# Delta rule's inversion: products, copies and masked writes over 32 of 64 columns per chunk

## The reference, cut to what matters

```
decay = jnp.tril(jnp.exp(jnp.tril(g[..., :, None] - g[..., None, :])))
tri = jnp.tril(jnp.einsum('bhnck,bhndk->bhncd', k_beta, k) * decay, -1)
eye = jnp.eye(chunk, dtype=jnp.float32)
Tm = jsl.solve_triangular(eye + tri, jnp.broadcast_to(eye, tri.shape), lower=True)
v_new = Tm @ v_beta
k_cum = Tm @ (k_beta * jnp.exp(g)[..., None])
```

## Time and profile before

| | |
|---|---|
| time, median of 3 runs | 3494.46 us (3492.59 to 3495.26) |
| profiled execution: its time, its span | 3488.75 us, 3487.0 us |
| busy: PE, PEld, DVE, ACT, POOL | 3025.8, 2083.1, 2289.0, 1233.2, 1019.2 us |
| mean granted TensorE clock | 0.944 of full speed |

### The profile page before, as it was taken

The page is one execution under the profiler, slowest core; times in us unless marked ns, Lnnn a source line. Parts: engine busy times, 40 slices in busy tenths (PEclk is TensorE's granted clock), DMA queues, the critical chain, the costliest instruction groups (busy, mean ns, idle before and its releaser), DMA issues. The chain is left out here.

```text
span 3487.0 us, 82116 instructions
## 1 busy us (share of the span) xinstructions
PE 3025.8 (87%) x33083; PEld 2083.1 (60%) x33083; DVE 2289.0 (66%) x5113; ACT 1233.2 (35%) x2979; POOL 1019.2 (29%) x1495
## 2 busy tenths in 40 slices
PE   6999998299966899889889889989989988988597
PEld 3444443166654677667667667667666766766365
DVE  4666666588835675775776666676677667665476
ACT  2333434033323333343343333333334234332354
POOL 3545556057821211212221221221221222121011
PEclk8999999599968999999999999999999999999799
DMA  2111111000001000010010010000000000000000
GB/s 80 32 33 32 34 31 27 30 1 1 1 14 39 23 25 18 17 29 20 17 29 18 19 29 17 20 18 28 20 17 29 20 17 29 17 17 2 25 19 31
DMA packets 94038, 80.40 MB, mean 23 GB/s; under 512 B 54992, under 2 KB 68320, under 8 KB 93664
## 3 DMA queue, kind: packets, MB, share of 16 engines
q1 hardware_dynamic: 93664, 75.18, 7.9%
HBM read 57.70 MB, written 4.85 MB: 18 GB/s over the span
## 5 line engine op out<-in xcount | busy, mean ns | idle before, releaser
L1643 PE MATMUL gd_bk<-gd_xT,gd_wh 128*128 128x512 f32 x768 | 416.0, 653 | 17.1 <-ACT gd_xT L1358 7.8
L1368 ACT COPY gd_O<-gd_bk 64x128 f32<-64x128 f32 x448 | 110.0, 259 | 561.2 <-PE gd_bk L1770 560.8
L1413 DVE SCALAR_TENSOR_TENSOR gd_YK<-gd_bk,gd_cw,gd_YK 128x511 f32<-128x511 f32 (+2 forms) x384 | 285.5, 743 | 18.5 <-ACT gd_YK L1290 11.9
L390 DVE TENSOR_REDUCE at_nm<-at_ring 128x2 f32<-128x256 f32 (+3 forms) x256 | 199.2, 820 | 145.9 <-PE at_ring L531 145.9
L1471 DVE COPY_PREDICATED gd_U<-gd_mU,gd_bk 128x256 f32<-128x256 int32 x320 | 140.9, 440 | 201.1 <-PE gd_bk L1836 138.3
L1379 ACT COPY gd_ZS<-gd_bk 128x256 f32<-128x256 f32 x320 | 119.1, 372 | 387.3 <-PE gd_bk L1814 379.6
L1814 PE MATMUL gd_bk<-gd_L,gd_NT 64*64 64x64 f32 x5120 | 203.7, 223 | 57.8 <-DVE gd_L L1473 57.8
L1814 PEld LDWEIGHTS gd_bk<-gd_L,gd_NT 64*64 64x64 f32 x5120 | 169.2, 134 | 112.5 <-DVE gd_L L1473 75.2
L1831 PE MATMUL gd_bk<-gd_U,gd_ZS 64*64 64x64 f32 x5120 | 203.4, 221 | 0.1
L276 POOL TENSOR_TENSOR at_PT<-at_PT,at_dm 128x1024 f32<-128x1024 f32 (+3 forms) x128 | 197.3, 1541 | 10.6
L1786 PE MATMUL gd_bk<-gd_V,gd_KK 64*128 64x128 f32 x896 | 165.8, 306 | 38.6 <-DVE gd_V L1564 38.2
(11 more groups left out here) (358 smaller groups left out, 6746.4 us busy)
## 6 DMA issues: line engine op xcount, KB each, us to landing
gd_wh<-in_L_attn_W_qkvz SPq DMA_DIRECT2D x64, 512.0 KB, 3.7
gd_gb<-gates SPq DMA_DIRECT2D x128, 64.0 KB, 3.3
X<-in_L_attn_x SPq DMA_DIRECT2D x8, 512.0 KB, 8.7
at_QT<-at_QS SPq DMA_DIRECT2D x128, 32.0 KB, 1.9
at_KT<-at_KS SPq DMA_DIRECT2D x128, 32.0 KB, 1.9
at_OC<-at_Ob SPq DMA_DIRECT2D x128, 32.0 KB, 1.9
at_RC<-inverse SPq DMA_DIRECT2D x128, 32.0 KB, 1.8
out_x<-X SPq DMA_DIRECT2D x8, 512.0 KB, 2.9
```

Of the source, the lines that this page charges most:

```text
L390: nc.vector.tensor_reduce(nm[v % 2][:, k, c0:c0 + HS + 1:HS], set_of(s, 2 + p)[:, :, 0:n], AX.X, ALU.max).then_inc(max_done, 1)
L1413: nc.vector.scalar_tensor_tensor(out[:, s:W], bank_[:, 0:W - s], cw[:, j, head(f, e), CONVK - 1 - s:CONVK - s], out[:, s:W], ALU.mult, ALU ...
L1643: ins = nc.tensor.matmul(out[:, :], wh[e][:, k, col * DK:(col + 1) * DK], xT[:, k, :], start=k == 0, stop=k == DC - 1)
```

## The change

At level l, `U` changes only in those columns whose index has bit l set (side 1), and `L` only in those where it is clear (side 0): 32 of 64 per chunk. The new helper `side` picks these columns out of a chunk as blocks of 2^l columns with as many skipped between them, `side_all` and `side_mask` do so for a whole tile, and `packed` and `packed_rows` address a part of the bank in which only such columns lie, side by side: 128 instead of 256 columns for a head. All products of the inversion now move 32 columns instead of 64, with the same 64 x 64 stationary operand; the ACT copy moves 128 x 128, and writes it in the places of side 0 of `ZS`; the masked writes on DVE are 128 x 128. The number of instructions in the inversion, their order and their semaphores stay as they are. `ZS` is set to zero once by POOL, with a wait for it on ACT; the masks are stored for four chunks (128 x 256) instead of one, since `side_mask` can't be broadcast.

```diff
@@ -877,6 +877,7 @@
     H, DK, CK = 8, P, 64
     CPT = P // CK
     NCH = N // CK
+    HC = CK // 2
     CONVK = conv_w.shape[2]
     LEVELS = 6
     W = TPS * P
@@ -900,8 +901,8 @@
         maskc, identc = sb("maskc", [P, CK]), sb("identc", [P, CK])
         jj, ii, jx = sb("jj", [P, CK], I32), sb("ii", [P, CK], I32), sb("jx", [P, CK], I32)
         m1, m2 = sb("m1", [P, CK], I32), sb("m2", [P, CK], I32)
-        mU = [sb(f"mU{l}", [P, CK], I32) for l in range(LEVELS)]
-        mL = [sb(f"mL{l}", [P, CK], I32) for l in range(LEVELS - 1)]
+        mU = [sb(f"mU{l}", [P, TPS, CK], I32) for l in range(LEVELS)]
+        mL = [sb(f"mL{l}", [P, TPS, CK], I32) for l in range(LEVELS - 1)]
         xs = sb("xs", [P, TPS, D])
         xT = sb("xT", [P, DC, W])
         mhalf = sb("mhalf", [P, 2 * TPS])
@@ -992,7 +993,8 @@
                         for src, dst in ((ii, mU[l]), (jj, mL[l] if l < LEVELS - 1 else None)):
                             if dst is not None:
                                 mask(nc.vector.tensor_scalar(m2[:, :], src[:, :], l, 1, ALU.logical_shift_right, ALU.bitwise_and))
-                                mask(nc.vector.tensor_tensor(dst[:, :], m1[:, :], m2[:, :], ALU.mult))
+                                mask(nc.vector.tensor_tensor(dst[:, :, :], m1[:, :].unsqueeze(1).broadcast_to([P, TPS, CK]),
+                                                             m2[:, :].unsqueeze(1).broadcast_to([P, TPS, CK]), ALU.mult))
                     dve.wait_ge(c_in, 6 * 16)
                     with dve.Fori(0, B) as b:
                         dve.wait_ge(gxt_mm, b * DC + 2)
@@ -1099,6 +1101,7 @@
             "z_mm", "zs_done", "y_mm", "u_done", "vk_mm", "kc_mm", "vnc_done", "kc_done", "oz_done")
         p1_mm, w_done, o1_done, ds_mm, s_done, oi_mm, o_done, ms_done, h_done, ht_mm, ht_out = per_head(
             "p1_mm", "w_done", "o1_done", "ds_mm", "s_done", "oi_mm", "o_done", "ms_done", "h_done", "ht_mm", "ht_out")
+        zs_zero = [sem(f"zs_zero{e}") for e in E2]
         gb_in = [[sem(f"gb_in{e}{i}") for i in range(2)] for e in E2]
         rk_step, rk_done, rq_step, rq_done, fac_step, fac_done = (
             sem(n) for n in ("rk_step", "rk_done", "rq_step", "rq_done", "fac_step", "fac_done"))
@@ -1153,6 +1156,26 @@
 
         def wide(m):
             return m[:, :].unsqueeze(1).broadcast_to([P, TPS, CK])
+        def side(ap, l, bit):
+            return ap.rearrange("p (b s n) -> p b s n", s=2, n=1 << l)[:, :, bit, :]
+        def side_all(tile, l, bit):
+            return tile[:, :, :].rearrange("p t (b s n) -> p (t b) s n", s=2, n=1 << l)[:, :, bit, :]
+        def side_mask(m, l, bit):
+            return m[:, :, :].rearrange("p t (b s n) -> p (t b) s n", s=2, n=1 << l)[:, :, bit, :]
+        def packed(b_, part, l):
+            return b_[:, part * TPS * HC:(part + 1) * TPS * HC].rearrange("p (b n) -> p b n", n=1 << l)
+        def packed_rows(b_, part, c, t, l):
+            return b_[rows(c), part * TPS * HC + t * HC:part * TPS * HC + (t + 1) * HC].rearrange("p (b n) -> p b n", n=1 << l)
 
         def ends_seq(q):
 
@@ -1266,6 +1289,8 @@
                     pool.wait_ge(eps_done, b + 1)
                     nc.gpsimd.tensor_tensor(rstd[:, :], rstd[:, :], mhalf[:, 0:TPS], ALU.pow).then_inc(rstd_done, 1)
 
+                for e in E2:
+                    nc.gpsimd.memset(ZS[e][:, :, :], 0.0).then_inc(zs_zero[e], 1)
                 exponents(0)
                 for q in range(-1, PAIRS):
                     f = q + 1
@@ -1376,7 +1401,9 @@
                         for e in E2:
                             if has(f):
                                 act.wait_ge(z_mm[e], f * (LEVELS - 1) + l)
-                                nc.scalar.copy(ZS[e][:, :, :], chunks(A_[e])).then_inc(zs_done[e], 1)
+                                if f == 0 and l == 1:
+                                    act.wait_ge(zs_zero[e], 1)
+                                nc.scalar.copy(side_all(ZS[e], l, 0), packed(A_[e], 0, l)).then_inc(zs_done[e], 1)
                         if l == 1 and has(f):
                             queries_first(f, 0)
                             if has(f + 1):
@@ -1462,15 +1489,15 @@
                 def first_level(f, e):
                     dve.wait_ge(nt_done[e], f + 1)
                     dve.wait_ge(ui_done[e], f + 1)
-                    nc.vector.copy_predicated(U[e][:, :, :], wide(mU[0]), NTm[e][:, :, :])
+                    nc.vector.copy_predicated(side_all(U[e], 0, 1), side_mask(mU[0], 0, 1), side_all(NTm[e], 0, 1))
                     dve.wait_ge(idz_mm[e], f + 1)
-                    nc.vector.copy_predicated(L[e][:, :, :], wide(mL[0]), chunks(F1[e])).then_inc(u_done[e], 1)
+                    nc.vector.copy_predicated(side_all(L[e], 0, 0), side_mask(mL[0], 0, 0), packed(F1[e], 0, 0)).then_inc(u_done[e], 1)
 
                 def level(f, e, l):
                     dve.wait_ge(y_mm[e], f * (LEVELS - 1) + l)
-                    last = nc.vector.copy_predicated(U[e][:, :, :], wide(mU[l]), chunks(A_[e], 1))
+                    last = nc.vector.copy_predicated(side_all(U[e], l, 1), side_mask(mU[l], l, 1), packed(A_[e], 2, l))
                     if l < LEVELS - 1:
-                        last = nc.vector.copy_predicated(L[e][:, :, :], wide(mL[l]), chunks(A_[e], 0))
+                        last = nc.vector.copy_predicated(side_all(L[e], l, 0), side_mask(mL[l], l, 0), packed(A_[e], 1, l))
                     last.then_inc(u_done[e], 1)
 
                 def attention_rows(f, e):
@@ -1708,7 +1735,7 @@
                     pe.wait_ge(nt_done[e], f + 1)
                     for t in range(TPS):
                         for c in range(CPT):
-                            last = nc.tensor.matmul(F1[e][rows(c), t * CK:(t + 1) * CK], NTm[e][rows(c), t, :], identc[rows(c), :],
+                            last = nc.tensor.matmul(packed_rows(F1[e], 0, c, t, 0), NTm[e][rows(c), t, :], side(identc[rows(c), :], 0, 0),
                                                     start=True, stop=True)
                     last.then_inc(idz_mm[e], 1)
 
@@ -1811,8 +1838,8 @@
                                     ge(pe, s_done[e], f * NCH)
                                 for t in range(TPS):
                                     for c in range(CPT):
-                                        last = nc.tensor.matmul(A_[e][rows(c), t * CK:(t + 1) * CK], NTm[e][rows(c), t, :], L[e][rows(c), t, :],
-                                                                start=True, stop=True)
+                                        last = nc.tensor.matmul(packed_rows(A_[e], 0, c, t, l), NTm[e][rows(c), t, :],
+                                                                side(L[e][rows(c), t, :], l, 0), start=True, stop=True)
                                 last.then_inc(z_mm[e], 1)
                         if l == 1 and has(f):
                             queries_in(f, 1)
@@ -1828,13 +1855,13 @@
                                 pe.wait_ge(zs_done[e], f * (LEVELS - 1) + l)
                                 for t in range(TPS):
                                     for c in range(CPT):
-                                        last = nc.tensor.matmul(A_[e][rows(c), (TPS + t) * CK:(TPS + t + 1) * CK], ZS[e][rows(c), t, :],
-                                                                U[e][rows(c), t, :], start=True, stop=True)
+                                        last = nc.tensor.matmul(packed_rows(A_[e], 2, c, t, l), ZS[e][rows(c), t, :],
+                                                                side(U[e][rows(c), t, :], l, 1), start=True, stop=True)
                                 if l < LEVELS - 1:
                                     for t in range(TPS):
                                         for c in range(CPT):
-                                            last = nc.tensor.matmul(A_[e][rows(c), t * CK:(t + 1) * CK], U[e][rows(c), t, :], ZS[e][rows(c), t, :],
-                                                                    start=True, stop=True)
+                                            last = nc.tensor.matmul(packed_rows(A_[e], 1, c, t, l), U[e][rows(c), t, :],
+                                                                    side(ZS[e][rows(c), t, :], l, 0), start=True, stop=True)
                                 last.then_inc(y_mm[e], 1)
                         if l == 4 and has(f):
                             values_across(f, 1)
```

## The result

The change makes the kernel slower. Its median is 3673.24 us (3669.5 to 3684.95, four runs), that of the kernel before beside it 3493.53 us (3487.43 to 3495.26, four runs): 1.0523 times the time, 95% interval 1.0495 to 1.0552, 180 us more. The forecast of 3442 and its range are both missed; what came is rival C, at over five times its price.

What follows compares the result with a forecast made beforehand. No engine bounded the whole inversion part: PE paced level 1 and from level 4's Z products on, DVE between. Steps summed to 1.67 us a pair, together 52 us, taking 3494.5 to 3442; range 3400 to 3490.

Steps and rivals of the forecast that it cites:

- rival C: Inversion part: PE streams half the columns, so its clock falls; 1.35 us a fall, two a pair give 3528 us; chance 0.09.
- The products. Here I expect almost nothing: Inversion products: the 64-column stationary operand keeps records 30 ns apart; only a group's last record ends about 0.03 us sooner.
- step 1: `queries_in` of head 0, waiting for a masked write, starts earlier, limited by head 1's transposes: gain 0.22 us a pair.
- step 2: End of level 1: head 1's writes end sooner, so level 2's taps and head 1's Z group start 0.30 us earlier.
- step 3: Level 2: both heads' shorter writes let the Z group of level 3 start another 0.54 us earlier.
- step 4: Level 3: both heads' writes stand on the path; Z of head 0 gains 0.27, head 1 another 0.20: 0.47 us.
- step 5: Level 4: PE sets the pace, so gain 0; the saved DVE time turns into DVE idle.
- step 6: Level 5: Y products follow the first ACT copy; 0.11 us from the copy and 0.03 from the drain give 0.14.
- Rival B: DVE's masked writes in short runs with gaps aren't shorter; some 0.2 us a pair remains, 3488 us; chance 0.08.
- Rival A: Inversion products get cheaper, 15 ns a record instead of 30; some 3.3 us a pair more, 3340 us; chance 0.06.
- The 0.03 that I took at each group's end: Last record of each product group, 223 ns, should shrink by about 0.03 us for 32 columns less.
- Costs taken as nothing: Mask products' 2.1 us on DVE covered by a 2.45 us wait for PE; POOL's zeroing of `ZS` hidden before pair 0's gates.

## Why the prediction was wrong

**The failed step** is "The products. Here I expect almost nothing". For the distance of the records it was right. But it took PE's price from the records alone and put the clock among the rivals at 0.09, with the reason that "weight loads, the busy share of PE and the gaps stay as they are". They did stay, and the clock fell all the same: in the 14.4 us ahead of the fall of pair 5 PE was busy for 12.51 us and loaded weights for 9.44, against 12.19 and 8.89 before; in the low stretch it was busy in 20.40 of 20.40 us, with a weight load for each record, and stayed at 0.50. What the runs put in place of that step is a fall of 20.4 us in 22 of the 32 parts and of about 10 in seven, 179 us net of the gain, that comes with the narrow products and with nothing else of the change. The row that could have told was in the prediction, 0.50 with PE busy for 31.3 of 36 us; 96 of its 142 records move 16 columns, the others 128. I read it as a clock that hadn't risen yet.

The Trainium skill, in TensorE: Matmul & The Clock Gate, Part 1, has the clock low by default and released by PE's activity. The busy share of the records can't be read as that activity here: it was 1.00 in the stretch at 0.50.

**Rival C** named the mechanism, the place and the sign. Its size was off, and the term that was off is the length of a fall. It took 1.35 us for one, from a scan part whose mean clock of 0.95 over 31.74 us comes to some 3.2 us at 0.50, and two falls a pair for 3528. What came was one of 20.4 us, which costs 8.7. For each us at the lower level that is about 0.42 us by the prediction's rows, and 0.43 and 0.42 in the falls of 20.4 and 10.2 us: the price was right, and a fall over six times as long made the loss. The prediction said "more if the clock stays down" and gave that no number.

**The steps of the sum.** For pair 14, at full clock in both kernels, I compared the starts of PE's groups counted from the start of the part. The gain had reached 0.06 us at the first `queries_in` (step 1 said 0.22); 0.16 at head 1's Z group of level 2 (step 2: another 0.30, got 0.10); 0.83 at head 1's Z group of level 3 (step 3: another 0.54, got 0.67); 1.08 at the Z groups of level 4 and 1.18 at the Y groups behind them (step 4: another 0.47, got 0.25 to 0.35); 1.20 at the Z groups and 1.33 at the Y groups of level 5 (step 5: 0; step 6: 0.14, got 0.13); 1.35 at the end. (The starts are good to 0.02.) So the path was right, and from level 2 on a write saved the 0.13 that it was priced at (0.33 to 0.20). Steps 1 and 2 fell short because their writes are those of levels 0 and 1. (Step 1 was too large besides, by an estimate from the rows before: the projection at 2022.81 starts 0.15 us after the last record of the group ahead of it, so the transposes alone would have left 0.08 of its 0.22.) With 1.35 for 1.67 a pair, and no falls, the forecast of 52 us would have been 43.

**Rival B** was right for levels 0 and 1: where the runs are of one or two columns the record isn't shorter, and only 0.04 to 0.10 us of the queue is saved. With runs of four columns it is wrong.

**Rival A** was wrong: 32 records of 32 columns took 1.12 us, against 1.15 for 64 columns. The 0.03 that I took at each group's end isn't there: in pair 14 a group of 16 that follows directly behind another of the same shape takes 0.63 us in both kernels. It comes once at the start of a group that follows other work (0.66 for 0.68, 1.12 for 1.15), and all products narrow save 0.19 us a part. The rule in the Trainium skill, TensorEngine Tiling (Array Packing), section Instruction Overhead, is that one free column has the same latency as 60. The trace agrees, with 64 for the wide ones: 221 ns for 32 columns against 223 for 64.

**Costs taken as nothing.** The mask chain on DVE took 11.5 us instead of 9.3, the 2.1 more that was forecast, but the wait for PE didn't cover all of it: the copy behind it now started 0.22 us after the chain, released by it, and 2.38 instead of 2.00 us after the start of PE's transposes. That is 0.4 us, once. The larger masks and the zeroing of `ZS` also stand in the kernels that are 27 to 43 us faster than before. (The writes of levels 4 and 5 are 6 of the 22 of a pair, not 8; the sum doesn't use the number.)

**What stays open.** What exactly the clock follows wasn't measured. Fewer moving columns at the same records and loads bring it down; a third or two thirds of the products narrow, or all but those of levels 2 and 3, don't. Pair 14 moves the same 637 records as pair 5 and keeps the clock, so the columns aren't the whole condition: why three of the 32 parts keep it wasn't found, nor why a masked write into runs of one or two columns takes longer; that it is the target's runs is argued from what the long ones share, as no kernel changed the target alone.

## What to carry to other kernels

Don't make the moving operand narrower than the stationary one for its own sake: here the records stayed as far apart, so PE gained next to nothing (0.19 us of 30), and the clock fell over a stretch in which PE looked fully busy. Narrow the copies and masked writes that read the result instead, out of the full-width bank, and leave the products as they are. When a fall of the clock is a rival, price it by each us at the lower level (about 0.42 us here, in the scan and in the inversion alike) and ask what a fall costs that lasts through most of the part that changes, not only one as short as those seen before. And look at the clock of each stage before reading busy times as a gain.

## What the hardware showed that was not expected

- The clock at 0.50 for 20.4 us with PE busy in all of them, 310 records and 310 weight loads in the stretch (pair 5); with the last two levels at 64 columns, 10.2 us.
- The price of the lower clock: 32 records of 32 columns took 1.12 us at 1.00 and 1.90 at 0.50; a part with a fall lost 0.42 us for each us of it.
- Gaps cost nothing on the PE and ACT side: products written in place with gaps took 221 ns a record, the ACT copy took 266 ns out of the packed bank and out of one with gaps, and the inversion part of pair 14 took 30.06 us with all results packed and with all in place.
- Masked writes of 128 elements took 0.44 to 0.50 us where the target lies in runs of one or two columns and 0.28 to 0.29 from runs of four on; those of 256 elements, without gaps, took 0.43 to 0.44.
